# The second layer's products of values in bursts of four steps in place of two, one step behind the scores in place of two

## The reference, cut to what matters

```
ss = sigmoid(x @ Ws), sd = sigmoid(x @ Wd)       # [t, H=8, E=5], top 3 of 5 kept: ss_g, sd_g, md
q  = einsum('bthed,bthe->bhtd', (x @ Wq), sd_g)  # D = 64
k, v likewise from x @ Wkv with ss_g
attn = softmax(q * scale @ k.T)                  # 8 heads, 2048 x 2048 each, not causal
out  = attn @ v
o5   = out @ Wo per expert; x + einsum('bthem,bthe->btm', o5, md)
```

## Time and profile before

| | |
|---|---|
| device time, median of 3 runs | 1695.55 us (1686.46 to 1697.53) |
| the profiled execution | 1687.58 us, its span 1685.8 us |
| PE busy in the span | 1556.2 us (92%) |
| DVE, ACT, POOL busy | 74%, 56%, 50% |
| matmuls of the values' products, L887 | 1024, of the page's 8404 |

### The profile page before, as it was taken

One profiled execution on the slowest core, in us unless ns is written; L12 is line 12 of the kernel. 1 busy time (PEld: TensorE's weight loads), 2 busy tenths in 40 slices (PEclk: granted clock), 3 DMA queues, 4 the chain that ended last, 5 costly groups with the idle time before them and its releaser, 6 DMA issues.

```text
span 1685.8 us, 27140 instructions
## 1 busy us (share of the span) xinstructions
PE 1556.2 (92%) x8404; PEld 1012.7 (60%) x8404; DVE 1254.2 (74%) x2518; ACT 939.7 (56%) x1582; POOL 847.9 (50%) x935
## 2 busy tenths in 40 slices
PE   4699999999999976689999999999999999999998
PEld 2455565565565545466666666567576666666555
DVE  3997787687679536777887778787778787777664
ACT  3446756756755631344655655655655656556652
POOL 2530000000001133458869879788689699698452
PEclk9599999999999987989999999999999999999998
DMA  2000000000000000000000000000000000000000
GB/s 64 0 1 1 2 1 2 1 1 1 1 1 1 1 12 13 1 1 13 0 13 1 1 13 2 0 13 1 13 1 1 13 1 1 1 1 1 1 7 19
DMA packets 12230, 9.39 MB, mean 6 GB/s; under 512 B 3840, under 2 KB 11584, under 8 KB 12096
## 3 DMA queue, kind: packets, MB, share of 16 engines
q1 hardware_dynamic: 12096, 7.66, 1.7%
HBM read 6.61 MB, written 1.05 MB: 5 GB/s over the span
## 4 chain that ended last, share of the span: by engine, by line
PE 63%; POOL 18%; DVE 9%; issue 4%; ACT 4%; SPq 1%; DMA 0%; DVEq 0%; ACTq 0%; POOLq 0%
PE ps L887 10%; PE ps L700 9%; PE ps L734 7%; PE ps L719 7%; PE ps L860 5%; PE ps L875 5%; POOL gs L1526 4%; PE ps L667 4%; PE ps L876 4%; POOL gsum L1527 3%; POOL z L572 3%; POOL onm L566 3%; PE ps L898 2%; POOL h_qk L1528 2%; DVE mxp L1201 2%
## 5 line engine op out<-in xcount | busy, mean ns | idle before, releaser
L1080 ACT ACTIVATE pbuf<-ps 128x512 f32<-128x512 f32 x512 | 301.6, 599 | 170.4 <-PE ps L876 166.2
L976 ACT ACTIVATE pbuf<-ps 128x1024 f32<-128x1024 f32 (+3 forms) x320 | 280.1, 897 | 182.5 <-PE ps L722 92.2
L1201 DVE TENSOR_REDUCE mxp<-ps 128x1 f32<-128x512 f32 (+2 forms) x432 | 279.1, 685 | 82.8 <-PE ps L700 51.4
L1407 DVE TENSOR_TENSOR den<-den,pbuf 128x1024 f32<-128x1024 f32 x224 | 312.8, 1396 | 1.9
L887 PE MATMUL ps<-pbuf,h_v 128*64 128x512 f32 x1024 | 248.7, 606 | 0.0
L1066 ACT ACTIVATE relu<-ps 128x512 f32<-128x512 f32 x256 | 152.2, 599 | 161.2 <-PE ps L860 132.1
L1359 DVE TENSOR_TENSOR gt<-ps,gate 128x320 f32<-128x320 f32 x384 | 181.6, 483 | 78.4 <-POOL h_v L1536 36.4
L700 PE MATMUL ps<-kM,qT 128*128 128x512 f32 (+3 forms) x640 | 230.9, 414 | 9.2 <-ACT kM L963 4.9
L875 PE MATMUL ps<-q1T,k1T 128*128 128x512 f32 x512 | 215.3, 421 | 11.4 <-ACT pbuf L1080 9.9
L1380 DVE CUSTOM_DVE_ANT_0 relu<-ps,relu 128x512 f32<-128x512 f32 x256 | 174.2, 684 | 64.5 <-PE ps L860 61.7
L719 PE MATMUL ps<-qT,kM 128*128 128x512 f32 (+3 forms) x640 | 199.5, 381 | 8.5 <-ACT pbuf L976 8.5
(11 more groups left out here) (224 smaller groups left out, 2799.5 us busy)
## 6 DMA issues: line engine op xcount, KB each, us to landing
wraw<-in_Wkv SPq DMA_DIRECT2D x16, 160.0 KB, 2.5
wraw<-in_Wq SPq DMA_DIRECT2D x8, 160.0 KB, 2.3
out<-x SPq DMA_DIRECT2D x4, 256.0 KB, 2.3
wqkv<-in_wqkvT SPq DMA_DIRECT2D x1, 192.0 KB, 3.9
masks<-in_masks SPq DMA_DIRECT2D x1, 128.0 KB, 4.1
dft<-in_dft SPq DMA_DIRECT2D x1, 128.0 KB, 2.3
wout<-in_Wo SPq DMA_DIRECT2D x2, 64.0 KB, 2.6
ident<-in_ident SPq DMA_DIRECT2D x1, 64.0 KB, 5.8
```

The source lines that it names most:

```text
L976: nc.scalar.activation(pbuf0[:, u % NP0, :, off:CH], ps[:, b:b + 2, off:CH], ACT.Exp, scale=float(D0) ** -0.5).then_inc(s_exp, 1)
L1080: nc.scalar.activation(pbuf1[:, u % NP1, i, :], ps[:, i, :], ACT.Exp, scale=float(D1) ** -0.5).then_inc(s_exp1, 1)
L1201: v.tensor_reduce(mxp[:, i, h:h + n, b], sc.rearrange("p (h k) -> p h k", h=n), AX.X, ALU.max).then_inc(s_read0d, 1)
L1407: v.tensor_tensor(dn, dn, w, ALU.add).then_inc(s_den1, 1)
```

## The change

A constant BURST = 4 and a new place for V and O. At a step u that is a multiple of four, right after its two scores, stand the products of u-4 to u-1; at a multiple of eight the copy O of the chunk follows at once, one step earlier than before. D and F keep their places.

```diff
+BURST = 4
...
             seq = [("S", 2 * u + half)] if u < U1 * H1 else []
             if half == 0:
                 return seq
+            if u % BURST == 0 and 0 < u <= U1 * H1:
+                seq += [("V", u - BURST + i) for i in range(BURST)]
+                if u % M1 == 0:
+                    seq.append(("O", u // M1 - 1))
             if 0 <= u - 2 < U1 * H1:
-                if u % 2:
-                    seq += [("V", u - 3), ("V", u - 2)]
                 seq.append(("D", u - 2))
-                if (u - 1) % M1 == 0:
-                    seq.append(("O", (u - 1) // M1 - 1))
             if 0 <= u - 4 < U1 * H1 and (u - 3) % M1 == 0:
                 seq.append(("F", (u - 3) // M1 - 1))
             return seq
```

## The result

The changed kernel takes 1724.24 us (1717.81 to 1729.39) where the kernel before takes 1695.91: ratio 1.0177 (of the means of four executions each; the two medians alone give 1.0167), 95% interval 1.0119 to 1.0235. It is slower, and outside the range that was given (1668 to 1706). The profiled executions, 1717.81 and 1687.58 us, stand 30.2 us apart, in spans of 1716.0 and 1685.8.

The account below looks back on a forecast made before the run. TensorE was taken to bound the kernel; -22.4 + 2 + 0 + 6 + 5 = -9.4 us took the profiled 1687.58 us to 1678, or 1686 on the median of 1695.55. The range was 1668 to 1706.

Parts of the forecast that it names:

- What bounds the kernel: Second-layer head: TensorE, busy 115.16 of 118.00 us, sets the pace and is bound by its own queue, not starved.
- The saving of 22.4 us: TensorE's switches between scores and products: bursts halve from 128 to 64, each saving 0.35 us.
- The moved products: Products one step earlier: no new waits of their own; transposes behind ScalarE's later casts cost +2 us (0 to +7).
- The lean stretches: Stretches without products, some four a head: ScalarE and VectorE waits add 0.8 us a head, 6 us in all.
- the dense part's 0.7: Steps 12 to 20, GpSimd full: two bursts' saving can't be had, 0.7 us a head, 5 us over seven heads.
- The clock: TensorE's granted clock in the layer: under 1.00 it would spoil all of the forecast; no size given.
- The fold: Second chunk's fold, the tightest case: about 0.3 us of slack left, 0 us taken, up to 8 us.
- The end: Products interleaved with the last zt and y: nothing waits for a shorter burst, 0 us.
- (B): Long stretches without products: ScalarE's and VectorE's feed becomes the bound, +19 us, 1715 us; chance 0.20.
- (A): TensorE's queue: the whole 22.4 us comes through because buffers absorb the longer bursts, 1673 us; chance 0.28.
- (C): Burst edges: TensorE's queue does not shorten, 0 saved, and unevenness leaves +8 us, 1704 us; chance 0.06.

Follow-up runs that it names:

- the runs with heads of 119.1 and 118.5 us: Changed kernel with transposes a whole step later (1707.69 us), and with those of heads 2 to 7 behind the next burst of four (1700.62 us).
- the mixed run: Changed kernel with bursts of four only in a head's first and last chunk, twos at odd steps in between: 1697.05 us, ratio 1.0008.

## Why the prediction was wrong, point by point

**What bounds the kernel: right, but read too far.** TensorE sets the pace, and its waits were 27 us. That it "is bound by its own queue, not starved" says how the old order stands, and not what holds it up: some bursts also stood where TensorE would otherwise have waited, as the row without a wait at 1069.76 shows.

**The saving of 22.4 us: right in its mechanism and size.** 64 runs of 16 products, edges of 0.33 and 0.34 us, 3.59 us each, and 0.32 us a switch between the one-step and two-step runs. (Over all bursts it is rather 0.34 us than 0.35, 22 us in all: bursts of 4, 8 and 16 matmuls take 1.01, 1.87 and 3.58 us to the next start, which is 0.15 us over 0.43 a pair each time, and some 0.09 us ahead and 0.10 behind come to it.) It is what leaves TensorE's queue; how much of it reaches the time depends on the waits. This is the term that "TensorEngine Tiling (Array Packing)" (Key Properties) bears on in the Trainium skill: a change of tiling mode drains the engine. The runs agree with that rule as far as a price per switch goes, 0.34 us whatever the burst's length; that it is a drain no row shows.

**The moved products: here the prediction failed.** The step reads "Their transposes wait today 4.8 us in 7 times; I give them +2 us over the layer (0 to +7, one microsecond a head)". Measured: +16 us for sk alone, 4.8 to 20.7, another 8 for the maxima in sq and 5 for free banks ahead of transposes. I had looked for new waits among the products' own semaphores and behind O, found none, and costed the place that the burst left at nearly nothing. But the change takes 1.87 us of TensorE work out of the way between the cast and the transpose in steps 22 to 24. The price could have been worked out from rows: the slack of each cross-engine step was that burst. The reason given for the +2 us, casts of ScalarE late behind its copy, wasn't the cause: the cast ended at 1075.0 and the transposes started at 1079.23, with VectorE between. The run with earlier low parts shows the holder, two sums on VectorE; the run with the transposes behind the burst shows the place.

The stretch that the prediction worked through, between the bursts of steps 20 and 24, shows the same error from the other side. It was put at 5.4 us and a stall of 0.7. It took 10.0 us (1070.75 to 1080.71), 2.8 of them idle. VectorE's three sums and two maxima took 5.6 us, just as reckoned, but they began only at 1071.98, since VectorE had stood idle during the burst; and the low parts behind them (1.07 us), named and not added in, were ready at 1079.17.

**The lean stretches.** "+0.8 us a head, 6 us in all" for ScalarE and VectorE, by way of the exponential: wrong mechanism. The score's wait for the exponential fell, 9.9 us to 1.7, in place of growing to 15 or 20. The unevenness is real, though: with the transposes covered (118.55 us) a head is still 2.4 us longer than 118.0 - 2.75 + 0.9 = 116.15 us, which the saved switches (eight at 0.34 us) and the phase alone would give. That is 2.4 us where 1.5 (0.8 and the dense part's 0.7) was put down. It is more, up to 3.3 us, if the phase's 0.9 was itself a cost of uncovered transposes. (In the bounds, 64 x 0.6 is 38, not 39.)

**The clock: not in the sum.** It stood only as something that "would spoil all of it". In every head from the second on the changed kernel has a fall of the granted clock at step 24, behind waits of 0.7, 0.3 and 1.8 us, and the second head has another at step 10, behind one of 1.4 us; a fall costs about 1.6 us. That waits bring the falls on is inferred from their order in the trace: here and with bursts of two each fall stands behind 1.3 us of waits or more. It isn't shown, and size alone doesn't decide: in the run with earlier low parts one fall (1.3 us) stands behind a single wait of 0.6 us; waits of 1.0 to 1.2 us in the runs with heads of 119.1 and 118.5 us brought none, and the same wait of 1.42 us in each of six heads of the mixed run brought three. Heads of equal instructions differ in it, so it isn't a function of the order alone.

**The fold**: right for the fold itself, which waited for GpSimd's denominator once, 0.6 us, at the very end. But the matmul behind it now waits 3.4 us in 6 times for the bank that VectorE's division holds, a wait that the list before doesn't have and the sum put at 0. **The end**: right, 22.1 us from the last score to the last matmul where it was 22.8.

The account of a head, in us: before 118.0; eight switches fewer, -2.75; one step of phase, +0.9 (bursts of two, even steps); transposes without cover, +2.75 (121.3, which is 122.9 less one fall, against 118.55); unevenness elsewhere, +2.4; one fall of the clock, +1.6. Sum 122.9. It comes out by construction, since the unevenness is what is left over, and is no proof of the terms. The first term comes from starts, the phase from a single head, and the 121.3 is an estimate; the phase opens waits of the same transposes, so it may be part of the uncovered transposes' 2.75 and leave more to unevenness. The split between the uncovered transposes and the unevenness rests on one edit, which moved the key differences as well. What of the 2.4 us belongs to banks, q2 or the exponential stays open. Bursts of four two steps behind, which would have parted length from phase the other way, weren't tried; with five probability buffers the exponential of step u waits for the products of step u-5, which would then stand behind that step's scores.

**The rivals.** (B) had the sign and about the size (1715), and its heads over 118 us, but its listed waits of 60 us or more came to 55, and it had the wrong queue: the engine that was late was VectorE, and the matmuls that waited were transposes, not scores. That its number came near is in part luck, since it held neither the transposes nor the clock. (A) is refuted; (C) too, by the edges.

## What to carry to other kernels

Before moving work on the engine that bounds, list for every step that it will now reach earlier how much slack its inputs have; a burst that costs switches may be the only thing that covers another engine's chain. Ask too what the other engines can do during a longer burst: VectorE stood idle through it and was late behind it. Merge bursts first where nothing from another engine is due between their old and new places: with three pairs of eight merged a head gained 0.8 us, with all eight it lost 4.9. It is a place to start and no law: with only two pairs merged, a head lost 0.2 us, for reasons left open.

Where a list of due times sets the order, move the consumers together with the cover, and judge by the length of a repeating unit at one granted clock rather than by the total.

## What the runs showed of the hardware

A fall of the granted clock costs about 1.6 us here (1.3 us in one case), and it can come in one of two heads that run the same instructions in the same order (117.19 and 118.76 us). The start of the second layer is moved by up to 11 us (718.1 or 728.9 us) with the granted clock ahead of it (0.80 or 0.72), where the kernels don't differ; this is as large as most effects that were studied. A burst of the values' products costs TensorE 0.34 us beyond its products where a full matmul follows it undisturbed, whether it holds 4, 8 or 16 matmuls.
